# Attention projections from 16-bit high and low parts, and the token transposes moved between the units of k

## The chip, the cores and the metric

The kernel runs on one core of a Trainium2 chip. The metric is the time of one execution on the device in microseconds, from runs of the same compiled program. The engines are called as the profile calls them: PE (TensorE, matmuls), PEld (its weight loads), DVE (VectorE), ACT (ScalarE), POOL (GpSimd) and SP (SyncE, which here only issues DMAs).

## The reference

128 graphs of 128 nodes and 384 features. Each graph is normalised, clipped at zero, and goes through masked attention with 12 heads of 32 features; the input is added to the result.

```python
h = jnp.maximum(_layernorm(x, axis=-1), 0.0)         # x: (128, 128, 384)
q, k, v = (split_heads(h @ W + b) for W, b in ((Wq, bq), (Wk, bk), (Wv, bv)))
scores = einsum('bhqd,bhkd->bhqk', q, k) / sqrt(32) + beta * adj
scores = where(adj > 0, scores, -9e15)
out = x + einsum('bhqk,bhkd->bhqd', softmax(scores), v)
```

All arrays are fp32, and the result is to be close to fp32 arithmetic.

## The kernel before

The graphs are taken four at a time: G = 4 graphs are 512 tokens, and 32 such groups are the steps. Step s projects group s and, in the same time, does the attention of group s-1. 33 steps run in all: step 0 has only projections, step 32 only attention. Each engine runs its own program, and only semaphores tie them together, so the order of instructions on an engine is what its `step` function writes out.

A step is cut into 12 slots, u = 0 to 11. In each slot one chunk of the attention is worked on: a chunk is one graph and CH = 3 chunks of four heads, so 12 chunks for a group. The chunk whose scores are made in slot u is u - 3 (LAG = 3); chunks 9 to 11 of a group thus come in slots 0 to 2 of the step after. A chunk goes through:

- PE: four matmuls into the one score bank `ps_s` (L456), which first waits for DVE to be done with the chunk before
- DVE: four fused instructions that add the mask and take the maximum (L638)
- ACT: four exps (L523)
- PE, one slot later: four transposes of the fp32 probabilities into `ps_t` (L464); ACT copies them as fp16 (L548), and DVE makes the low part, `ps_t` minus that copy, in fp16 (L644)
- PE, a slot later still: twelve small matmuls with v's high and low parts (L479 to L481). After the third chunk of a graph DVE takes the reciprocal of the sums (L654) and scales (L659), POOL adds the input and v's bias (L334), and SP stores

The order on DVE within a slot: L638 for chunk n, then the low parts of the units that PE ended in the slot before (`low_parts`), the reciprocal, one graph's statistics of the next group (L586), the scaling, the mask of the next group (L598 in slot 4, L603 in slot 7), the aggregation of the statistics (L592), and last L644 for chunk n-1. The order on ACT: the exps of chunk n, L548 for chunk n-1, then the high parts of what PE ended in this slot.

Between these, PE works through 13 units, listed in UNITS: three of q, three of k (each 128 output columns for 512 tokens), four of v (one graph each), and three turns. A turn transposes 128 of the 384 normalised features of the next group (L415), and ACT (L530, with the clip at zero) and DVE (L609) split it into a high and a low part, `hT`. A projection unit is 9 matmuls (L435): three blocks of 128 features, each as high x high, low x high and high x low, with both parts kept in fp32 storage as fp32r, which PE multiplies at reduced precision. For q and k the weights are stationary and 512 tokens stream; for v the tokens are stationary and 384 columns stream. ATOMS and PIECES share the 13 units out over the 24 halves of slots by columns (512 or 384 a matmul, 1024 a turn; 44544 in all). Units rotate through three PSUM banks `ps_p`; before a unit starts, `bank_free` waits for what empties the bank's last user: DVE's low part for q, k and turns, ACT's copy for v. The high parts of q and k are made by ACT (L543) and the low ones by DVE (L619), both in fp16; SP spreads them by 12 DMAs each over `q_st` and `k_st` (L248), which the scores read.

POOL computes 1/sqrt(variance) for the next group (L302 to L305) once all its statistics are in, normalises its four graphs (L313), adds v's bias to the input (L319), splits v (L326, L328) and makes the final additions.

Of the kernel before, what the change touches and what calls it, by code (L numbers as in the profile page):

```python
# [5 lines left out]
F32 = mybir.dt.float32  # L6
# [9 lines left out]
EPS = 1e-5  # L16
MASKED = -9000000000000000.0
EXPONENT = 0x7F800000
BINADE = 1 << 23


def graph_attention_kernel(nc, x, adj, wq, bq, wk, bk, wv, bv, beta, out):
# [17 lines left out]
    assert N == P and TOK == 512 and HPC * N == 512  # L40


    UNITS = ([("q", c) for c in range(CH)] + [("k", c) for c in range(CH)]
             + [("v", 0), ("v", 1), ("turn", 0), ("v", 2), ("turn", 1), ("v", 3), ("turn", 2)])
    NB = len(UNITS)
    PROJ = [u for u in UNITS if u[0] != "turn"]
    QK = 2 * CH
    NP = len(PROJ)


# [33 lines left out]
    with ExitStack() as ctx:  # L84
# [3 lines left out]
        def sem(name):  # L88
            return ctx.enter_context(nc.semaphore(name))

        w = sb("w", [P, 2, CH, 3 * D], F32R)
        ones = sb("ones", [P, P], BF16)
        ident = sb("ident", [P, P], F32)
        b_row = sb("b_row", [P, 2, D], F32)
# [18 lines left out]
        rstd = sb("rstd", [P, G], F32)  # L113
        hn = sb("hn", [P, G, D], F32)

        hT = sb("hT", [P, 2, 2, CH, TOK], F32R)
        qT = sb("qT", [P, 2, CH, TOK], FP16)
        kT = sb("kT", [P, 2, CH, TOK], FP16)
        q_st = sb("q_st", [P, 2, HPC, CH, TOK], FP16)
# [167 lines left out]
        @block.gpsimd  # L287
        def _(pool):
            pool.memset(ident[:], 0.0).then_inc(ident_zeroed, 1)
            pool.memset(ones[:], 1.0).then_inc(consts_set, 1)  # L290
            pool.wait_ge(ident_zeroed, 1)
            pool.affine_select(out=ident[:], in_=ident[:], compare_op=ALU.not_equal, fill=1.0, base=0,
                               pattern=[[-1, P]], channel_multiplier=1).then_inc(consts_set, 1)
            pool.memset(half[:], -0.5).then_inc(consts_set, 1)
            pool.wait_ge(consts_set, 3)

            def rstd_of(s):

                wait(pool, var_done, G * (s + 1))
                wait(pool, normed, G * s)  # L300
                pool.nop(nofuse=True)
                pool.tensor_scalar(var_eps[:], mean_var[:, :, 1], EPS, None, ALU.add).then_inc(eps_added, 1)  # L302
                pool.tensor_scalar(neg_mean[:], mean_var[:, :, 0], -1.0, None, ALU.mult).then_inc(eps_added, 1)
                pool.wait_ge(eps_added, 2 * (s + 1))
                pool.tensor_tensor(rstd[:], var_eps[:], half[:], ALU.pow).then_inc(rstd_done, 1)  # L305

            def normalise(s, par):

                pool.wait_ge(rstd_done, s + 1)
                wait(pool, h_turned, CH * s)  # L310
                pool.nop(nofuse=True)
                for j in range(G):
                    pool.tensor_scalar(hn[:, j, :], xs[:, par, j, :], neg_mean[:, j:j + 1], rstd[:, j:j + 1],  # L313
                                       ALU.add, ALU.mult).then_inc(normed, 1)

            def add_bias(s, par, j):
                wait(pool, x_in[par], 8 * (s - par) + 16)
                wait(pool, added, G * (s - 2) + j + 1)
                pool.tensor_tensor(xb[:, par, j, :], xs[:, par, j, :], bv_row[:], ALU.add).then_inc(xb_done, 1)  # L319

            def split_v(s, par, j):
                wait(pool, pv_done, SLOTS * (s - 2) + CH * (j + 1))
                pool.wait_ge(v_copied, G * s + j + 1)
                pool.nop(nofuse=True)
                v32 = v_f[:, j % 2].rearrange("p (h d) -> p h d", d=HD)
                pool.tensor_copy(v1[:, par, j, :, 0:HD], v32).then_inc(v_high, 1)  # L326
                pool.wait_ge(v_high, G * s + j + 1)
                pool.tensor_tensor(v2[:, par, j], v32, v1[:, par, j, :, 0:HD], ALU.subtract).then_inc(v_split, 1)  # L328

            def add_x(s, par, j):  # L330

                pool.wait_ge(scaled, G * s + j + 1)
                pool.wait_ge(xb_done, G * s + j + 1)
                pool.tensor_tensor(on[:, j % 2, :], on[:, j % 2, :], xb[:, par, j, :], ALU.add).then_inc(added, 1)  # L334

            def step(s, par):
                proj, attend = 0 <= s <= STEPS - 1, 1 <= s <= STEPS
                older = 2 <= s <= STEPS
                if 1 <= s <= STEPS:
                    split_v(s - 1, 1 - par, G - 1)  # L340
                if proj:
                    add_bias(s, par, 0)
                    add_bias(s, par, 1)
                if older:
                    add_x(s - 2, par, 2)
                if proj:
                    add_bias(s, par, 2)
                if 0 <= s <= STEPS - 2:
                    rstd_of(s + 1)
                    normalise(s + 1, 1 - par)  # L350
                if older:
                    add_x(s - 2, par, 3)
                if proj:
                    add_bias(s, par, 3)
                if attend:
                    add_x(s - 1, 1 - par, 0)
                if proj:
                    split_v(s, par, 0)
                    split_v(s, par, 1)
                if attend:  # L360
                    add_x(s - 1, 1 - par, 1)
                if proj:
                    split_v(s, par, 2)
                if s == STEPS:
                    add_x(s - 1, 1 - par, 2)
                    add_x(s - 1, 1 - par, 3)

            rstd_of(0)
            normalise(0, 0)
            w_c = w_raw[:, :, W_COLS[1]]  # L370
            pool.wait_ge(w_squared, 2)
            pool.wait_ge(qk_scaling, 9)
            pool.tensor_tensor(w_c, w_c, gap[:, 1:2, :].bitcast(F32).broadcast_to([P, CH, D]),
                               ALU.mult).then_inc(wk_scaled, 1)
            pool.wait_ge(w_squared, 3)
            pool.wait_ge(v_scaling, 6)
            for c in range(CH):
                w_c = w_raw[:, c, W_COLS[2]].rearrange("p (h d) -> p h d", d=HD)
                pool.tensor_tensor(w_c, w_c, v_scale[:].rearrange("p (h o) -> p h o", o=1).broadcast_to([P, HEADS, HD]),
                                   ALU.mult).then_inc(wv_scaled, 1)  # L380
            for par in range(2):
                for j in range(G):
                    pool.tensor_copy(v1[:, par, j, :, HD], v_scale[:]).then_inc(consts_set, 1)
            pool.wait_ge(bv_in, 16)
            run_steps(step)

        @block.tensor
        def _(pe):
            def bank_free(s, par, o):
# [14 lines left out]
                if kind == "turn":  # L404
                    wait(pe, h_low, CH * (before + 1) + n + 1)
                elif kind == "v":
                    wait(pe, v_copied, G * before + n + 1)
                else:
                    wait(pe, qk_low, QK * before + last + 1)

            def turn(s, bank, c):

# [102 lines left out]
        def _(act):  # L515
# [52 lines left out]
                act.activation(w_sq[:, n], w_raw[:, :, W_COLS[n]], ACT.Square).then_inc(w_squared, 1)  # L568
            def weights_high(n, ready, count):
                act.wait_ge(ready, count)  # L570
                act.activation(w[:, 0, :, W_COLS[n]], w_raw[:, :, W_COLS[n]], ACT.Copy).then_inc(w_high, 1)

            weights_high(0, wq_scaled, 1)
            for c in range(CH):
# [7 lines left out]
        def _(dve):  # L582
# [23 lines left out]
            def turn_low(s, par, bank, c):  # L606

                dve.wait_ge(h_high, CH * s + c + 1)
                dve.scalar_tensor_tensor(out=hT[:, par, 1, c, :], in0=bank[:], scalar=0.0,  # L609
                                         in1=hT[:, par, 0, c, :].bitcast(F32), op0=ALU.max,  # L610
                                         op1=ALU.subtract).then_inc(h_low, 1)

            def low_part(s, par, o):

                kind, n = UNITS[o]
                bank = ps_p[BANK[par][o]]
                dve.wait_ge(qk_high, QK * s + o + 1)
                dst, b = (qT, 0) if kind == "q" else (kT, 1)
                dve.scalar_tensor_tensor(out=dst[:, 1, n, :], in0=bank[:], scalar=bias_qk[:, b, n:n + 1],  # L619
                                         in1=dst[:, 0, n, :], op0=ALU.add, op1=ALU.subtract).then_inc(qk_low, 1)  # L620
# [42 lines left out]
            def step(s, par):  # L663
                proj, ahead = 0 <= s <= STEPS - 1, 0 <= s <= STEPS - 2
                for u in range(SLOTS + (LAG + 3 if s == STEPS else 0)):
# [7 lines left out]
                        low_parts(s - 1, 1 - par, SLOTS - 1, s <= STEPS - 1)  # L673
                    if ended:
                        invert_sums(valued[1], valued[3] // CH)
                    if ahead and u < G:
                        moments(s + 1, 1 - par, u)
                    if ended:
                        scale_out(valued[1], valued[3] // CH)
                    if proj and u == 4:  # L680
                        mask_unlinked(s, par)
                    if proj and u == 7:
                        mask_linked(s, par)
                    if ahead and u < G:
                        variance(s + 1, u)
                    if turning:
                        p_low(turning[0], (u - LAG - 1) % 2)

# [33 lines left out]
                              ALU.mult).then_inc(b_scaled_done, 1)  # L722
            def weights_low(n):
                dve.wait_ge(w_high, n + 1)
                dve.tensor_tensor(w[:, 1, :, W_COLS[n]], w_raw[:, :, W_COLS[n]], w[:, 0, :, W_COLS[n]].bitcast(F32),
                                  ALU.subtract).then_inc(w_low, 1)

            turn_low(0, 0, ps_h[0], 0)
            weights_low(0)
# [47 lines left out]
```

## Time and profile before

| | before |
|---|---|
| time, median of 3 runs | 1162.26 us (1161.06 to 1162.73) |
| time of the profiled execution | 1160.99 us |
| its span, first to last instruction | 1159.1 us |
| mean granted TensorE clock | 0.974 |
| busy: PE, PEld, DVE, ACT, POOL | 94%, 78%, 84%, 77%, 50% |
| DMA | 138.79 MB, mean 120 GB/s |

A busy share is the union of an engine's instructions over the span. PE's instructions are pipelined, so they overlap and a busy PE may still be waiting for the next one; DVE and ACT show the length of each instruction with its latency, and the start of the next one may lie before the end of the one before. The distance of two starts is therefore the better measure of what one instruction costs, and it is used throughout.

### The profile page before, as it was taken

Reading aid. Unit: us, or ns where it says so; the run is one execution under the profiler, and the core shown is the slowest. Engines: PE = TensorE matmul, PEld = TensorE weight load, DVE = VectorE, ACT = ScalarE, POOL = GpSimd, SP = SyncE. Lnnn points to the kernel's source line nnn. Section 1 sums busy time; section 2 is a strip of 40 time slices with the busy share of each in tenths; the row PEclk is TensorE's granted clock in tenths of the full one; section 3 lists DMA queues with packets and bytes.
Section 4 is the critical chain, followed back from the end, with each engine's and each line's share of the span. In section 5 each row is a group of like instructions: output and inputs, shape, how many; then the busy total and the mean of one; then the engine's idle time right before and its main releaser. Section 6 shows DMA issues by size and latency. Waiting matters only on the chain. (4 is left out here: it accounts for less than half of the span.)

```text
span 1159.1 us, 33776 instructions
## 1 busy us (share of the span) xinstructions
PE 1089.7 (94%) x10959; PEld 902.9 (78%) x10959; DVE 972.2 (84%) x4343; ACT 891.0 (77%) x2343; POOL 578.6 (50%) x756
## 2 busy tenths in 40 slices
PE   4899999999999999999999999999999999999986
PEld 2778878888878888787888887888888788888764
DVE  6578888888888888898888888888889888888865
ACT  2377888788787888787888878788877888887865
POOL 3735464454555454546545455545454554545331
PEclk9999999999999999999999999999999999999965
DMA  4444434554434455444455443445544444543320
GB/s 145 116 123 123 110 105 123 140 147 126 120 98 123 130 140 136 120 111 113 119 137 147 130 116 100 122 128 139 145 115 109 114 119 134 147 126 98 98 70 28
DMA packets 91038, 138.79 MB, mean 120 GB/s; under 512 B 15600, under 2 KB 66288, under 8 KB 90864
## 3 DMA queue, kind: packets, MB, share of 16 engines
q1 hardware_dynamic: 90336, 135.85, 43.7%
q8 instruction: 88, 1.44, 0.6%
q14 instruction: 86, 0.70, 0.2%
q10 hardware_dynamic: 528, 0.79, 0.2%
HBM read 35.91 MB, written 25.17 MB: 53 GB/s over the span
## 5 line engine op out<-in xcount | busy, mean ns | idle before, releaser
L523 ACT ACTIVATE probs<-biased,neg_max 128x128 f32<-128x128 f32 x1536 | 491.9, 391 | 222.8 <-DVE neg_max L638 186.0
L435 PE MATMUL ps_p<-hT,w 128*128 128x512 f32 x1728 | 527.1, 423 | 5.2 <-DVE qT L619 2.5
L644 DVE TENSOR_TENSOR pT<-ps_t,pT 128x512 f16<-128x512 f32 x384 | 262.9, 685 | 141.3 <-ACT pT L548 141.0
L334 POOL TENSOR_TENSOR on<-on,xb 128x384 f32<-128x384 f32 x128 | 129.2, 1009 | 471.8 <-DVE on L659 392.9
L638 DVE CUSTOM_DVE_ANT_0 biased<-ps_s,mask 128x128 f32<-128x128 f32 x1536 | 352.0, 285 | 6.3 <-PE ps_s L456 4.3
L435 PEld LDWEIGHTS ps_p<-hT,w 128*128 128x128 f32 x1728 | 294.2, 192 | 53.4 <-DVE hT L609 7.3
L435 PE MATMUL ps_p<-w,hT 128*128 128x384 f32 x1152 | 270.2, 357 | 30.4 <-DVE hT L609 30.4
L464 PE MATMUL ps_t<-ident,probs 128*128 128x128 f32 x1536 | 237.8, 279 | 3.1 <-ACT probs L523 1.5
L464 PEld LDWEIGHTS ps_t<-ident,probs 128*128 128x128 f32 x1536 | 193.9, 143 | 43.8 <-ACT probs L523 7.1
L548 ACT ACTIVATE pT<-ps_t 128x512 f16<-128x512 f32 x384 | 220.5, 574 | 1.2 <-PE ps_t L464 1.2
L435 PEld LDWEIGHTS ps_p<-w,hT 128*128 128x128 f32 x1152 | 186.8, 189 | 37.6 <-DVE hT L609 37.5
L479 PEld LDWEIGHTS ps_o<-v,pT 128*128 128x128 f16 x1536 | 122.8, 96 | 84.7 <-issue 73.9
L479 PE MATMUL ps_o<-v,pT 128*128 128x33 f16 x1536 | 160.3, 181 | 3.2 <-DVE pT L644 2.3
L456 PE MATMUL ps_s<-k_st,q_st 96*128 96x128 f16 x1536 | 150.7, 221 | 7.4 <-DVE neg_max L638 4.9
L481 PE MATMUL ps_o<-v,pT 128*128 128x32 f16 x1536 | 155.6, 177 | 0.0
L480 PE MATMUL ps_o<-v,pT 128*128 128x33 f16 x1536 | 155.6, 178 | 0.0
L319 POOL TENSOR_TENSOR xb<-xs,bv_row 128x384 f32<-128x384 f32 x128 | 128.8, 1017 | 8.9 <-POOL on L334 0.4
L638 DVE DVE_READ_ACCUMULATOR2_ANT neg_max<- 128x1 f32 x1536 | 127.7, 83 | 0.1
L480 PEld LDWEIGHTS ps_o<-v,pT 128*128 128x128 f16 x1536 | 125.5, 97 | 0.3
L481 PEld LDWEIGHTS ps_o<-v,pT 128*128 128x128 f16 x1536 | 124.1, 96 | 0.0
L328 POOL TENSOR_TENSOR v<-v_f,v 128x384 f16<-128x384 f32 x128 | 114.0, 891 | 10.3
L456 PEld LDWEIGHTS ps_s<-k_st,q_st 96*128 96x128 f16 x1536 | 90.5, 97 | 10.6 <-DVE neg_max L638 6.2
(62 smaller groups left out, 1034.9 us busy)
## 6 DMA issues: line engine op xcount, KB each, us to landing
q_st<-qT SPq DMA_DIRECT2D x384, 96.0 KB, 2.2
k_st<-kT SPq DMA_DIRECT2D x384, 96.0 KB, 2.2
out<-on SPq DMA_DIRECT2D x128, 192.0 KB, 2.1
xs<-in_x SPq DMA_DIRECT2D x31, 768.0 KB, 4.8
adjs<-in_adj SPq DMA_DIRECT2D x32, 256.0 KB, 5.1
xs<-in_x ACTq DMA_DIRECT2D x1, 768.0 KB, 7.6
k_st<-in_L_gnn_Wq SPq DMA_DIRECT2D x1, 576.0 KB, 5.9
k_st<-in_L_gnn_Wk SPq DMA_DIRECT2D x1, 576.0 KB, 9.2
```

The lines of the kernel that those rows point to most:

```text
L319: pool.tensor_tensor(xb[:, par, j, :], xs[:, par, j, :], bv_row[:], ALU.add).then_inc(xb_done, 1)
L334: pool.tensor_tensor(on[:, j % 2, :], on[:, j % 2, :], xb[:, par, j, :], ALU.add).then_inc(added, 1)
L435: mm = pe.matmul(dst, stationary, moving, start=m == 0, stop=m == MMS - 1)
L456: mm = pe.matmul(ps_s[:, i * N:(i + 1) * N], q_st[0:STACK, gp, i, c, j * N:(j + 1) * N], k_st[0:STACK, gp, i, c, j * N:(j + 1) * N], start ...
L464: mm = pe.transpose(ps_t[odd][:, i * N:(i + 1) * N], probs[:, odd, i, :], ident[:])
L479: pe.matmul(o, high, first, start=True, stop=False)
L480: pe.matmul(o, low, first, start=False, stop=False)
L481: mm = pe.matmul(o[:, 0:HD], high, second, start=False, stop=True)
L523: act.activation(probs[:, odd, i, :], biased[:, odd, i, :], ACT.Exp, bias=neg_max[:, odd, i:i + 1], scale=-1.0).then_inc(exp_done, 1)
L548: act.activation(pT[:, odd, 0], ps_t[odd][:].rearrange("p (h q) -> p h q", q=N), ACT.Copy).then_inc(p_high_done, 1)
L638: dve.tensor_tensor_reduce(out=biased[:, odd, i, :], in0=ps_s[:, i * N:(i + 1) * N], in1=mask[:, gp, v // CH, :], scale=-1.0, scalar=3.0e3 ...
L644: dve.tensor_tensor(pT[:, odd, 1], ps_t[odd][:].rearrange("p (h q) -> p h q", q=N), pT[:, odd, 0], ALU.subtract).then_inc(p_low_done, 1)
```

## The change

The high and low parts of the weights (`w`) and of the tokens (`hT`) are kept in fp16. So that small low parts keep their bits, weights are multiplied by SHRINK = 4 when they are split, and tokens are divided by 4: the variance is multiplied by 16 before the power of -1/2. The products stay as they were. The numbers of matmuls, and the columns in them, stay too. The three turns stand behind k0, k1 and k2 in UNITS instead of between and after the units of v; QK_AT keeps the count of q and k units right. On POOL the 1/sqrt and the normalisation come before `add_x` of graph 2 and `add_bias` of graph 2. On DVE the statistics and their aggregation for four graphs are done two each in slots 0 and 1, where it was one each in slots 0 to 3.

```diff
+SHRINK = 4.0
...
-    UNITS = ([("q", c) for c in range(CH)] + [("k", c) for c in range(CH)]
-             + [("v", 0), ("v", 1), ("turn", 0), ("v", 2), ("turn", 1), ("v", 3), ("turn", 2)])
+    UNITS = ([("q", c) for c in range(CH)] + [(kind, c) for c in range(CH) for kind in ("k", "turn")]
+             + [("v", j) for j in range(G)])
...
+    QK_AT = {o: [u for u in UNITS if u[0] in "qk"].index(unit) for o, unit in enumerate(UNITS) if unit[0] in "qk"}
...
-        w = sb("w", [P, 2, CH, 3 * D], F32R)
+        w = sb("w", [P, 2, CH, 3 * D], FP16)
...
-        hT = sb("hT", [P, 2, 2, CH, TOK], F32R)
+        hT = sb("hT", [P, 2, 2, CH, TOK], FP16)
...
-                pool.tensor_scalar(var_eps[:], mean_var[:, :, 1], EPS, None, ALU.add).then_inc(eps_added, 1)
+                pool.tensor_scalar(var_eps[:], mean_var[:, :, 1], SHRINK * SHRINK, SHRINK * SHRINK * EPS, ALU.mult,
+                                   ALU.add).then_inc(eps_added, 1)
...
+                if 0 <= s <= STEPS - 2:
+                    rstd_of(s + 1)
+                    normalise(s + 1, 1 - par)
                 if older:
                     add_x(s - 2, par, 2)
                 if proj:
                     add_bias(s, par, 2)
-                if 0 <= s <= STEPS - 2:
-                    rstd_of(s + 1)
-                    normalise(s + 1, 1 - par)
...
-                    wait(pe, qk_low, QK * before + last + 1)
+                    wait(pe, qk_low, QK * before + QK_AT[last] + 1)
...
-                act.activation(w[:, 0, :, W_COLS[n]], w_raw[:, :, W_COLS[n]], ACT.Copy).then_inc(w_high, 1)
+                act.activation(w[:, 0, :, W_COLS[n]], w_raw[:, :, W_COLS[n]], ACT.Copy, scale=SHRINK).then_inc(w_high, 1)
...
-                                         in1=hT[:, par, 0, c, :].bitcast(F32), op0=ALU.max,
+                                         in1=hT[:, par, 0, c, :], op0=ALU.max,
...
-                dve.wait_ge(qk_high, QK * s + o + 1)
+                dve.wait_ge(qk_high, QK * s + QK_AT[o] + 1)
...
-                    if ahead and u < G:
-                        moments(s + 1, 1 - par, u)
+                    if ahead and u < 2:
+                        for j in range(2 * u, 2 * u + 2):
+                            moments(s + 1, 1 - par, j)
...
-                    if ahead and u < G:
-                        variance(s + 1, u)
+                    if ahead and u < 2:
+                        for j in range(2 * u, 2 * u + 2):
+                            variance(s + 1, j)
...
-                dve.tensor_tensor(w[:, 1, :, W_COLS[n]], w_raw[:, :, W_COLS[n]], w[:, 0, :, W_COLS[n]].bitcast(F32),
-                                  ALU.subtract).then_inc(w_low, 1)
+                dve.scalar_tensor_tensor(out=w[:, 1, :, W_COLS[n]], in0=w_raw[:, :, W_COLS[n]], scalar=SHRINK,
+                                         in1=w[:, 0, :, W_COLS[n]], op0=ALU.mult, op1=ALU.subtract).then_inc(w_low, 1)
```

## Rows read from the trace of the kernel before

**Rows 1.** The page's part 1: busy us, share of the span, instructions.
```profile
PE 1089.7 (94%) x10959; PEld 902.9 (78%) x10959; DVE 972.2 (84%) x4343; ACT 891.0 (77%) x2343; POOL 578.6 (50%) x756
```

**Rows 2.** Windows: length, busy PE PEld DVE ACT POOL, clock, DMA: 31 steps; last 11 slots.
```profile
60.21:1119.41 1059.20, 1024.34 (x10544) 855.61 (x10542) 916.36 (x4164) 850.84 (x2257) 541.60 (x702) 0.99 0.46 123
1119.41:1150.02 30.61, 24.62 (x221) 16.20 (x220) 18.95 (x106) 19.34 (x55) 2.99 (x3) 0.50 0.08 27
```

**Rows 3.** Timeline of DVE near the end: start, length, engine, line, operation, [idle before].
```profile
1121.59 0.69 DVE L644 TENSOR_TENSOR pT<-ps_t,pT 128x512 f16<-128x512 f32 x1 [1.25 <-ACT pT L548]
1122.19 0.28 DVE L638 CUSTOM_DVE_ANT_0 biased<-ps_s,mask 128x128 f32<-128x128 f32 x1
```

**Rows 4.** Timeline of ACT in the same slot.
```profile
1119.80 1.28 ACT L523 ACTIVATE probs<-biased,neg_max 128x128 f32<-128x128 f32 x4 [1.02 <-DVE neg_max L638]
1120.98 0.57 ACT L548 ACTIVATE pT<-ps_t 128x512 f16<-128x512 f32 x1
```

**Rows 5.** Timeline of DVE in slot u=8.
```profile
519.14 0.28 DVE L638 CUSTOM_DVE_ANT_0 biased<-ps_s,mask 128x128 f32<-128x128 f32 x1
...
519.98 0.75 DVE L619 SCALAR_TENSOR_TENSOR kT<-ps_p,bias_qk,kT 128x512 f16<-128x512 f32 x1
520.65 0.22 DVE L654 RECIPROCAL inv_sum<-ps_o 128x12 f32<-128x12 f32 x1
...
521.38 0.68 DVE L644 TENSOR_TENSOR pT<-ps_t,pT 128x512 f16<-128x512 f32 x1
```

**Rows 6.** Windows of slots inside steps: u=2; u=6; u=7; u=10; u=11, 0, 1.
```profile
501.97:505.14 3.17, 3.17 (x30) 2.46 (x30) 3.17 (x15) 2.34 (x6) 0.50 (x1) 1.00 0.02 5
...
513.57:516.36 2.79, 2.79 (x31) 2.23 (x29) 1.53 (x11) 2.33 (x6) 1.59 (x2) 1.00 0.65 155
516.36:519.14 2.78, 2.78 (x33) 2.58 (x31) 2.78 (x12) 2.33 (x6) 0.00 (x0) 1.00 0.59 153
524.76:527.67 2.91, 1.95 (x26) 1.56 (x25) 2.22 (x11) 2.75 (x8) 1.25 (x2) 1.00 0.64 155
527.67:536.06 8.39, 8.39 (x87) 6.92 (x86) 7.66 (x36) 6.81 (x19) 5.65 (x7) 1.00 0.40 104
```

**Rows 7.** Timeline of PE in slot u=3 of that step.
```profile
504.19 0.38 PE L456 MATMUL ps_s<-k_st,q_st 96*128 96x128 f16 x4
504.38 0.95 PE L435 MATMUL ps_p<-hT,w 128*128 128x512 f32 x3
505.17 0.60 PE L464 MATMUL ps_t<-ident,probs 128*128 128x128 f32 x4
505.52 1.18 PE L435 MATMUL ps_p<-hT,w 128*128 128x512 f32 x4
```

**Rows 8.** Timeline of DVE in slot u=0: low part of turn 2, one graph's statistics.
```profile
531.31 0.69 DVE L609 SCALAR_TENSOR_TENSOR hT<-ps_p,hT 128x512 fp32r<-128x512 f32 x1
531.91 0.55 DVE L586 BATCH_NORM_STATS2 stats<-xs 128x6 f32<-128x384 f32 x1
532.55 0.18 DVE L592 BATCH_NORM_AGGREGATE mean_var<-stats 128x2 f32<-128x6 f32 x1
532.65 0.69 DVE L644 TENSOR_TENSOR pT<-ps_t,pT 128x512 f16<-128x512 f32 x1
```

**Rows 9.** Timeline of PE in slot u=10 and the start of u=11.
```profile
526.34 0.61 PE L435 MATMUL ps_p<-w,hT 128*128 128x384 f32 x2 [0.96 <-DVE hT L609]
527.11 0.38 PE L456 MATMUL ps_s<-k_st,q_st 96*128 96x128 f16 x4
```

**Rows 10.** Timeline of POOL in slots u=3 to 5.
```profile
507.65 0.24 POOL L302 TENSOR_SCALAR var_eps<-mean_var 128x4 f32<-128x4 f32 x1 [0.85 <-DVE mean_var L592]
...
509.55 2.81 POOL L313 TENSOR_SCALAR hn<-xs,neg_mean,rstd 128x384 f32<-128x384 f32 x4 [0.21 <-POOL rstd L305]
```

**Rows 11.** Timelines at the start: SP's issue of k's spreading, PE's first scores.
```profile
49.20 7.53 SPq L248 DMA_DIRECT2D k_st<-kT  x12
...
59.64 0.38 PE L456 MATMUL ps_s<-k_st,q_st 96*128 96x128 f16 x4 [2.53 <-DMA k_st<-kT]
```

## What the change does to the time, predicted before it was run

> **What bounds the kernel now.** I read the page first, then the windows, then the timelines of VectorE (DVE), ScalarE (ACT) and TensorE (PE), slot by slot. On the page PE is busy 94% of the span, DVE 84%, ACT 77% [rows 1]. That invites the reading that PE is the bound. The windows speak against it. The last 11 slots of the kernel have attention and no projection at all. PE has 221 instructions there, against 10544 in the 31 steps before, and its granted clock is 0.50, and yet they take 30.61 us, 2.78 us a slot. The 31 steps with projections take 1059.20 us, 34.17 us a step or 2.85 us a slot [rows 2]. So almost nothing of a slot's length comes from the projections. What sets it is a ring of waits between DVE and ACT, seen bare in one slot of that end: the mask-and-maximum group (L638) starts at 1119.41, where the window begins, the four exps (L523) at 1119.80, ACT's copy of the turned probabilities (L548) at 1120.98, DVE's low part of them (L644, after 1.25 us idle "<-ACT") at 1121.59, the next L638 at 1122.19 [rows 2 to 4]. That is 0.39 + 1.18 + 0.61 + 0.60 = 2.78 us. ACT does the copy of chunk n-1 only behind the exps of chunk n, and DVE the next L638 only behind that L644, so the ring closes without PE.
>
> In a step with projections the same 2.78 us stands under each slot, and a slot is longer only where something exceeds it. Name a slot by the step's own count u (0 to 11); its start is DVE's first L638, and the chunk scored there is u-3. DVE needs 0.84 us for L638 (519.14 to 519.98 [rows 5]) and 0.60 for L644, so 2.78 - 1.44 = 1.34 us fit between them for nothing. In [rows 6] slots u=6 and u=7 take 2.79 and 2.78, u=10 takes 2.91, u=11, 0 and 1 together 8.39 (2.80 each), and u=2 takes 3.17 with DVE busy throughout. Twelve bare slots would be 33.4 us; a step is 34.17 on the mean. Only those 0.8 us a step, and the start and end, are open to this change.
>
> **The change on PE.** First the projections. A run of three fp32 matmuls of 512 columns takes 505.17 - 504.38 = 0.79 us to the next group; one more lengthens the busy time from 0.95 to 1.18, so 0.23 us is one, and the first of a run costs 0.79 - 0.46 = 0.33 [rows 7]. Four fp16 scores of 128 columns take 504.38 - 504.19 = 0.19, which is 0.05 each, so I estimate 0.20 to 0.22 us for 512 fp16 columns and no surcharge for the first. For a step (54 such matmuls, 36 of 384 columns, 24 runs) that is about 54 x 0.02 + 36 x 0.01 + 24 x 0.10 = 3.8 us less work for PE. Its bounds are 0 and 5 us. All of it lies beside the ring. The value for the time is zero, except where PE catches up late: u=11, 0 and 1, where I take 0.05 us a step for all three (8.39 against 3 x 2.78).
>
> By the Trainium skill, page TensorE: Matmul & The Clock Gate, section Back-to-back issue gap, a warm matmul of 512 columns issues every 216 ns; no run so far shows it for fp16, and with it the saving would be about the same. The skill's page Perfetto Trace Analysis, section Identifying the Most-Contended Engine, would rank engines by busy share, with weight loads standing for TensorE. Here that gives DVE at 84% ahead of the weight loads at 78%, but neither share tells of the ring, and the rows decide. By that rule an unchanged total of DVE work would mean an unchanged time, 1162 us.
>
> **The turns move.** Counting columns (44544 a step in 24 halves), before has turn 0 to 2 in u=9, 10 and 11; after has turn 0 in u=5, turn 1 in u=6 and turn 2 in u=8. DVE's low part of a turned chunk (L609, 0.60 us: 531.31 to 531.91 [rows 8]) comes one slot later: before in u=10, 11 and 0, after in u=6, 7 and 9.
> - u=10 loses its stall. There v3 needs the bank of turn 0; PE waits 0.96 us for L609, starts at 526.34, and its scores at 527.11 let the next L638 start only at 527.67 [rows 6, 9]. The slot goes from 2.91 to 2.78: -0.13 us.
> - The same stall reappears in u=6. k2 needs the bank of turn 0, whose L609 is in u=6. PE starts k2 1.58 us into the slot as at u=10 (526.34 - 524.76), has two matmuls there too, of 0.22 each, which is about what two fp32 ones of 384 columns take with the surcharge of the first, and so the slot grows as u=10 did, from 2.79 to 2.91: +0.12 us. Bounds: 0 if the wait just fits, 0.25 if the first matmul keeps its surcharge.
> - u=7 gets three pieces of DVE work: low part of k1 (L619), L609 of turn 1, and the second half of the mask (L603). The slot is full already without L609 (DVE busy for 2.78 of its 2.78 us [rows 6]), so L609's 0.60 comes on top: 3.38 us, +0.60. Bounds 0.55 and 0.65; if fp16 made L609 half as long, 0.3. SP's load of adjs waits for that mask, but behind it SP would wait for an output addition anyway.
> - ACT in u=6 has the high part of k1 and the copy of turn 1; at u=10, with a high part of v and such a copy, it was busy for 2.75 of 2.91 us [rows 6]. k's high part is longer than v's, so this may bind by a little; I take 0, bounds 0 and 0.1.
>
> **The statistics move.** u=2 loses one of the four: it keeps L638, L619, the reciprocal and the scaling (520.65 to 521.38, 0.73) and L644, the same as slot u=8 has now: 0.84 + 0.67 + 0.73 + 0.60 = 2.84 us [rows 5]. It was 3.17: -0.33 us. u=3 loses its statistics as well, worth 0 to 0.07; I take 0.04. Slots 0 and 1 get two each: at most 0.55 + 0.64 + 0.10 = 1.29 us from [rows 8], under the 1.34 that fit, and u=0 has lost the L609 it had. Nothing.
>
> **GpSimd and the queues.** rstd and normalise come before add_x of graph 2 and add_bias of 2. They start when all statistics are in, now in u=1, and turn 0 needs them in u=5, over 10 us on; they take 4.7 us (507.65 to 512.36 [rows 10]). add_x 2, until now in u=3, may come 2 us later; SP's store of it stands ahead of the spreading of q, which waits for q2's low part in u=4 anyway. The variance's multiplication by 16 rides in an instruction that is there already. Nothing, bounds 0 and 0.1 a step.
>
> **The sum.** Per step -0.05 - 0.13 + 0.12 + 0.60 - 0.33 - 0.04 = +0.17 us. It holds for the 30 steps that look ahead and have attention: +5 us. The bounds: -0.3 a step (L609 at half length, no stall in u=6, and u=3 worth 0.07) to +0.4, so -9 to +12 us. At the start, attention waits for the spread of k, issued at 49.20 behind that of q; scores start at 59.64 [rows 11]. The four statistics now stand in pairs ahead of q's low parts and overlap a little, which I put at -0.6 us. Against it, k1 and k2 now stand behind turn 0, which in step 0 waits for GpSimd; I find k2's low part done just before SP is free, so 0, at worst +2. Scaling the weights while splitting them costs the same number of instructions. The end has no projections: nothing. In all 5.1 - 0.6 = +4.5, say +4 us. The profiled execution took 1160.99 us for a span of 1159.1; the median of the three runs lies 1.3 us above it. 1160.99 + 4 = 1165, and 1162.26 + 4 = 1166. I give 1166.
>
> **Rivals.**
> - PE is the bound after all. For it: 94% busy. Against it: the 30.61 us of the last 11 slots. It would give 3.8 us x 31 = 118 us less, 1044 us; chance 0.03.
> - The ring itself gets shorter, since fp16 operands disturb ACT and DVE less. For it: slots with projections show 2.79 to 2.80 instead of 2.78. Against it: that is all there is to gain. 12 x 0.025 = 0.3 us a step, 9 us in all, so 1166 - 9 = 1157; chance 0.14.
> - The two moves cancel: L609 costs less in u=7 than 0.60, or u=6 does not stall. It would give 1160 to 1164, no change; chance 0.18.
> - PE's clock drops, as it now has gaps in each slot. For it: the clock was 0.50 in the last slots, where PE waits for the ring [rows 2]. Against it: in u=10 PE was busy for 1.95 of 2.91 us at clock 1.00 [rows 6], and after the change it would be busy for 2.3 to 2.5 us of nearly every slot. It decides from the point where PE's work at half clock, some 7 projections x 0.44 + 1.9 = 5 us, exceeds the 2.78 of a slot; with two such slots a step it gives 2 x 2.2 x 30 = 132 us, about 1295 us; chance 0.03.
> - Turn 0 holds k up at the start, with the rest as forecast: 1168; chance 0.05.
>
> **How the numbers follow.** The forecast has the remaining 0.57. About 0.2% (2.3 us) is what a measurement of this kernel can tell from no change, so 1160 to 1164.6 is "same". Of the forecast 0.48 lies above and 0.09 in it; the shorter ring is 0.09 faster and 0.05 same; cancelling 0.02 faster, 0.13 same, 0.03 slower. With PE as bound (0.03 faster), the clock (0.03) and the start (0.05) slower, that is 0.14 faster, 0.27 same, 0.59 slower. The range 1157 to 1171 leaves out PE as bound, the clock, and the outer ends of the bounds of both signs.
>
> **What would show it.** In the changed profile: matmuls of 512 columns at about 0.22 us with no surcharge on the first, and PE idle in most slots, waiting for neg_max L638; the last 11 slots still 30.6 us; slot u=2 down to about 2.84, u=10 to 2.78, u=7 up to about 3.39 with DVE busy throughout, u=6 near 2.9 with PE waiting for L609. The prediction is wrong if u=7 stays near 2.8, if plain slots leave 2.78, or if the clock falls below 1.00 inside the steps.

## The result and the profile after

The changed kernel takes 1163.85 us (median of 20 runs, 1162.93 to 1164.96) against 1161.3 us for the kernel before in the same comparison: a ratio of 1.0021, with a 95% interval of 1.0015 to 1.0027. It is slower by a fifth of a per cent, 2.5 us. The profiled execution has a span of 1162.2 us, 3.1 more than before.

The page of the changed kernel, part 1 (compare [rows 1]):

```profile
PE 1050.3 (90%) x10959; PEld 721.8 (62%) x10959; DVE 978.9 (84%) x4343; ACT 892.0 (77%) x2343; POOL 567.9 (49%) x756
```

The weight loads of PE have lost 181 us of busy time and its matmuls 39, and the kernel is slower. DVE's and ACT's shares have hardly moved. The windows, cut at the same events as in [rows 2] and [rows 6] (length, busy PE, PEld, DVE, ACT, POOL, clock, DMA): the 31 steps; the last 11 slots; u=2; u=6; u=7; u=10; u=11, 0 and 1.

```profile
58.98:1122.39 1063.41, 985.57 (x10544) 685.24 (x10541) 923.55 (x4163) 851.83 (x2257) 530.96 (x700) 1.00 0.46 122
1122.39:1153.07 30.68, 24.60 (x221) 16.20 (x220) 18.94 (x107) 19.41 (x55) 2.99 (x3) 0.50 0.08 27
501.99:504.82 2.83, 2.83 (x31) 2.00 (x30) 2.80 (x14) 2.34 (x6) 2.54 (x5) 1.00 0.03 6
513.23:516.12 2.89, 1.59 (x23) 0.98 (x22) 2.22 (x11) 2.50 (x7) 1.55 (x2) 1.00 0.65 156
516.12:519.49 3.37, 3.37 (x38) 2.61 (x36) 3.37 (x13) 2.65 (x7) 0.00 (x0) 1.00 0.64 151
525.12:527.91 2.79, 2.79 (x33) 2.04 (x31) 1.53 (x11) 2.14 (x6) 1.39 (x3) 1.00 0.62 148
527.91:536.28 8.37, 8.03 (x84) 5.38 (x83) 7.71 (x39) 6.63 (x18) 7.16 (x11) 1.00 0.42 107
```

A step is now 34.30 us (1063.41 / 31) instead of 34.17. u=7 has grown from 2.78 to 3.37 with DVE busy throughout, u=6 from 2.79 to 2.89; u=2 has shrunk from 3.17 to 2.83, u=10 from 2.91 to 2.79. What fills u=7 is read from the timeline of DVE there (start, length, engine, line, operation):

```profile
516.12 0.29 DVE L642 CUSTOM_DVE_ANT_0 biased<-ps_s,mask 128x128 f32<-128x128 f32 x1
...
516.97 0.75 DVE L623 SCALAR_TENSOR_TENSOR kT<-ps_p,bias_qk,kT 128x512 f16<-128x512 f32 x1
517.63 0.68 DVE L613 SCALAR_TENSOR_TENSOR hT<-ps_p,hT 128x512 f16<-128x512 f32 x1
518.23 0.75 DVE L607 SCALAR_TENSOR_TENSOR mask<-adjs,beta_col,mask 128x512 f32<-128x512 f32 x1
518.89 0.69 DVE L648 TENSOR_TENSOR pT<-ps_t,pT 128x512 f16<-128x512 f32 x1
519.49 0.29 DVE L642 CUSTOM_DVE_ANT_0 biased<-ps_s,mask 128x128 f32<-128x128 f32 x1
```

Each starts as the one before it lets go: 0.85 + 0.66 + 0.60 + 0.66 + 0.60 = 3.37 us. (Lines are four further down than before: L642 was L638, L648 was L644, L613 was L609, L607 was L603, L439 was L435.) The low part of turn 1 takes 0.60 us as it did in fp32. And PE in u=6 waits for the bank of turn 0, then goes on with the scores of the next chunk at 515.56, which DVE takes up 0.56 us later, at 516.12 (start, length, ..., number of instructions in the group, [idle time before it <- what ended it]):

```profile
514.81 0.61 PE L439 MATMUL ps_p<-hT,w 128*128 128x512 f16 x2 [1.30 <-DVE hT L613]
515.56 0.38 PE L460 MATMUL ps_s<-k_st,q_st 96*128 96x128 f16 x4
515.78 0.81 PE L439 MATMUL ps_p<-hT,w 128*128 128x512 f16 x3
516.43 0.60 PE L468 MATMUL ps_t<-ident,probs 128*128 128x128 f32 x4
516.87 1.03 PE L439 MATMUL ps_p<-hT,w 128*128 128x512 f16 x4
```

### The profile page after: what moved, and what is told of

Read it like the earlier page. It is cut to its first block and busy times, and to the rows that moved or that the text cites. A ratio compares the mean times of both kernels' runs of the same rounds, so it can differ in the third digit from the quotient of the medians.

```text
span 1162.2 us, 33776 instructions
## 1 busy us (share of the span) xinstructions
PE 1050.3 (90%) x10959; PEld 721.8 (62%) x10959; DVE 978.9 (84%) x4343; ACT 892.0 (77%) x2343; POOL 567.9 (49%) x756
## 5 line engine op out<-in xcount | busy, mean ns | idle before, releaser
L439 PE MATMUL ps_p<-hT,w 128*128 128x512 f16 x1728 | 459.0, 382 | 62.0 <-DVE hT L613 38.6
L648 DVE TENSOR_TENSOR pT<-ps_t,pT 128x512 f16<-128x512 f32 x384 | 264.5, 689 | 147.0 <-ACT pT L552 143.6
L642 DVE CUSTOM_DVE_ANT_0 biased<-ps_s,mask 128x128 f32<-128x128 f32 x1536 | 351.7, 286 | 3.5 <-PE ps_s L460 2.5
L338 POOL TENSOR_TENSOR on<-on,xb 128x384 f32<-128x384 f32 x128 | 127.5, 996 | 416.7 <-DVE on L663 416.7
L439 PEld LDWEIGHTS ps_p<-hT,w 128*128 128x128 f16 x1728 | 155.1, 98 | 168.3 <-DVE hT L613 45.9
L439 PE MATMUL ps_p<-w,hT 128*128 128x384 f16 x1152 | 234.4, 326 | 1.3
L483 PEld LDWEIGHTS ps_o<-v,pT 128*128 128x128 f16 x1536 | 132.1, 96 | 48.5 <-DVE pT L648 7.6
L483 PE MATMUL ps_o<-v,pT 128*128 128x33 f16 x1536 | 156.8, 179 | 3.7 <-DVE pT L648 2.8
L484 PE MATMUL ps_o<-v,pT 128*128 128x33 f16 x1536 | 155.6, 178 | 0.0
L484 PEld LDWEIGHTS ps_o<-v,pT 128*128 128x128 f16 x1536 | 125.2, 97 | 35.3
L439 PEld LDWEIGHTS ps_p<-w,hT 128*128 128x128 f16 x1152 | 104.9, 98 | 55.6 <-DVE hT L613 9.6
L323 POOL TENSOR_TENSOR xb<-xs,bv_row 128x384 f32<-128x384 f32 x128 | 127.6, 1008 | 8.9 <-POOL on L338 0.4
L642 DVE DVE_READ_ACCUMULATOR2_ANT neg_max<- 128x1 f32 x1536 | 129.1, 84 | 0.0
L485 PEld LDWEIGHTS ps_o<-v,pT 128*128 128x128 f16 x1536 | 124.1, 96 | 0.0
L330 POOL CAST v<-v_f 128x384 f16<-128x384 f32 x128 | 64.8, 507 | 112.7 <-issue 102.8
```

The costliest lines, as they stand in the source:

```text
L439: mm = pe.matmul(dst, stationary, moving, start=m == 0, stop=m == MMS - 1)
L483: pe.matmul(o, high, first, start=True, stop=False)
L484: pe.matmul(o, low, first, start=False, stop=False)
L485: mm = pe.matmul(o[:, 0:HD], high, second, start=False, stop=True)
L642: dve.tensor_tensor_reduce(out=biased[:, odd, i, :], in0=ps_s[:, i * N:(i + 1) * N], in1=mask[:, gp, v // CH, :], scale=-1.0, scalar=3.0e3 ...
L648: dve.tensor_tensor(pT[:, odd, 1], ps_t[odd][:].rearrange("p (h q) -> p h q", q=N), pT[:, odd, 0], ALU.subtract).then_inc(p_low_done, 1)
```

## The experiments

The theory is the prediction's: a ring between DVE and ACT sets each slot at 2.78 us, and only what exceeds it counts. The main rival is that PE, 90 to 94% busy, is the bound. All ratios are against the kernel before, run on the same chip beside each.

**The fp16 parts alone.** The kernel before with the storage changed (with the factor 4, which is not shown below) and nothing moved:

```diff
-        w = sb("w", [P, 2, CH, 3 * D], F32R)
+        w = sb("w", [P, 2, CH, 3 * D], FP16)
-        hT = sb("hT", [P, 2, 2, CH, TOK], F32R)
+        hT = sb("hT", [P, 2, 2, CH, TOK], FP16)
...
```

> The kernel before with nothing changed but the storage of w and hT (fp16, with the factor 4); turns, statistics and POOL order as before. My theory, the ring of waits between DVE and ACT: every slot keeps its length (u=2 3.17, u=10 2.91, u=7 2.79), except u=11, 0 and 1, where PE was late, which lose up to 0.02 each; with the start, 1 to 3 us less than before, about 1159.5. Rival, PE is the bound: 54 x 0.02 + 36 x 0.01 = 1.4 us a step less, 45 us in all, about 1117. Rival, fp16 operands shorten the ring itself: plain slots under 2.78.

Measured 0.9942 (0.993 to 0.9955), 6.6 us less, against the 1 to 3 expected. Slot u=10, which I had left at 2.91, is shorter. Its timeline on PE, and its window:

```profile
521.70 0.50 PE L437 MATMUL ps_p<-w,hT 128*128 128x384 f16 x2 [1.14 <-DVE hT L611]
522.35 0.38 PE L458 MATMUL ps_s<-k_st,q_st 96*128 96x128 f16 x4
```

```profile
520.12:522.91 2.79, 1.65 (x25) 1.15 (x24) 2.14 (x12) 2.63 (x8) 1.25 (x2) 1.00 0.64 151
```

PE still waits for turn 0's low part and starts 1.58 us into the slot, as in [rows 9]. But from there to the scores it takes 0.65 us (521.70 to 522.35) where it took 0.77, and that is what the slot had over 2.78. So the stall was long enough to show only with fp32 parts: 0.12 x 30 = 4 us. Slots u=0 and u=1 lose 0.06 us a step together (means over the steps), some 2 us. The rest is at the start: the first L638 comes 1.0 us earlier and the first step with attention is 1.3 us shorter, in part as in the changed kernel (below). That makes some 8 us, the difference of the two profiled spans (1159.1 and 1151.1). The saving of PE as a whole (1.4 us a step at the least, 45 us) is not there: the rival of PE as the bound falls.

**The moves alone.** The changed kernel with both tensors back in fp32r.

> The changed kernel with w and hT in fp32 again (no factor 4); turns behind k0, k1, k2, statistics two in u=0 and 1, and POOL order stay changed. Ring theory: u=7 3.37 and u=6 2.89 to 2.95, u=2 2.83, so some 5 us slower than before in the steps, less what fp16 gave at the start: 1163 to 1168. Rival, the loss comes from the fp16 parts: then this kernel is at or under before, 1161.

Measured 1.0075 (1.0062 to 1.0088), 9 us slower, at 1168.47 the upper end of what was expected. Windows of u=6 and u=7:

```profile
516.15:519.19 3.04, 2.62 (x30) 1.97 (x29) 2.22 (x12) 2.65 (x7) 1.57 (x2) 1.00 0.63 151
519.19:522.56 3.37, 3.37 (x36) 2.84 (x35) 3.37 (x13) 2.50 (x7) 0.00 (x0) 1.00 0.59 145
```

u=7 is 3.37 in fp32 too, so its length doesn't come from the type. u=6 is 3.04 instead of 2.89, the same effect of the type as above. The two halves of the change multiply to 0.9942 x 1.0075 = 1.0017, which agrees with the 1.0021 of the whole: the change is a gain of 0.6% from the fp16 parts and a loss of 0.75% from the moves (turns, statistics and POOL's order together).

**The turns put back.** The changed kernel with the old order of units:

```diff
-    UNITS = ([("q", c) for c in range(CH)] + [(kind, c) for c in range(CH) for kind in ("k", "turn")]
-             + [("v", j) for j in range(G)])
+    UNITS = ([("q", c) for c in range(CH)] + [("k", c) for c in range(CH)]
+             + [("v", 0), ("v", 1), ("turn", 0), ("v", 2), ("turn", 1), ("v", 3), ("turn", 2)])
```

> The changed kernel with UNITS as before (turns between the units of v), all else changed. Ring theory: u=7 back to 2.79 and u=6 to 2.79, u=10 up to 2.91, but u=0 now has the low part of turn 2 beside two statistics, 0.84 + 0.60 + 1.16 + 0.60 = 3.20: per step 34.29 - 0.58 - 0.10 + 0.12 + 0.41 = 34.14, about 1159. Rival, the moved turns were for the good and something else costs: slower than 1164.

Measured 0.9948 (0.9935 to 0.996), the same as fp16 alone, and faster than the 1159 us that I expected, in part as u=10 did not go back to 2.91. Slots of one step: u=7 2.79, u=10 2.79, u=0 3.21. So of the moves it is the turns that cost. Moving the statistics, with POOL's order moved too, trades u=2 (3.17 to 2.83) for u=0 (2.79 to 3.21), where turn 2's low part meets two statistics. POOL's order was never changed alone.

**The masks out of the full slot.** The changed kernel with the mask in u=3 and 4:

```diff
-                    if proj and u == 4:
+                    if proj and u == 3:
                         mask_unlinked(s, par)
-                    if proj and u == 7:
+                    if proj and u == 4:
                         mask_linked(s, par)
```

> The changed kernel with the two halves of the mask in u=3 and u=4 instead of u=4 and u=7. Ring theory: u=7 has 0.84 + 0.67 + 0.60 + 0.60 = 2.71 of DVE work and falls from 3.37 to 2.79; u=4 has 0.84 + 0.67 + 0.68 + 0.60 = 2.79 and stays; 0.58 x 31 = 18 us less than the changed kernel, about 1146, under both. Rival, u=7 is long for PE or ACT (two units end in u=6): it stays near 3.3 and the time near 1163.

Measured 0.9909 (0.9894 to 0.9924), 1149.27 us. u=7 is 2.79 as expected, but u=3 grew to 2.91, which was not. The timelines of DVE and of POOL in that slot:

```profile
501.19 0.88 DVE L602 TENSOR_SCALAR mask<-adjs 128x512 f32<-128x512 f32 x1
501.99 0.68 DVE L648 TENSOR_TENSOR pT<-ps_t,pT 128x512 f16<-128x512 f32 x1
```

```profile
499.52 1.30 POOL L317 TENSOR_SCALAR hn<-xs,neg_mean,rstd 128x384 f32<-128x384 f32 x2
500.79 1.00 POOL L338 TENSOR_TENSOR on<-on,xb 128x384 f32<-128x384 f32 x1
```

L602 takes 0.88 us instead of 0.42, and it ends 0.28 us after POOL's L338 does (501.19 + 0.88 = 502.07 and 500.79 + 1.00 = 501.79). So I left L602 in u=4 and moved only L607, to u=6:

> The changed kernel with only the mask's second half (L607) moved, from u=7 to u=6; L602 stays in u=4. With both halves in u=3 and 4, u=3 had grown to 2.90, as L602 took 0.88 us there instead of 0.42 while POOL was at its own L317 and L338. If POOL's work beside it does that, L602 is back to 0.42, u=3 to 2.79, u=6 stays 2.89 (0.84 + 0.60 + 0.68 + 0.60 = 2.72 of DVE work), u=7 2.79: 33.67 a step, some 1146 us, 3 below the version with the masks in u=3 and 4. Rival: L602 is slow in any slot after the move: 1149 or more.

Measured 0.9868 (0.9853 to 0.9883), 1144.86 us, as expected. L602 over all 32 steps, shortest, median and longest in ns, in the version with u=3 and in this one:

```profile
L602 DVE TENSOR_SCALAR mask<-adjs x32: 417/878/1025, 37.4 to 1075.8; 128x512 f32<-128x512 f32 x32
```

```profile
L602 DVE TENSOR_SCALAR mask<-adjs x32: 414/417/1141, 38.0 to 1073.5; 128x512 f32<-128x512 f32 x32
```

With one DVE instruction moved by one slot the changed kernel is 1.3% faster than before instead of 0.2% slower. This is the price of u=7 measured directly: 3.37 - 2.79 = 0.58 us a step, with u=6 still at 2.89.

**Less work for PE.** The kernel before with five of the nine matmuls of each projection unit left out (q, k and v lack most of their low-part products):

```diff
                 for m in range(first, end):
+                    if m % 3 and m != MMS - 1:
+                        continue
```

> The kernel before with 4 of the 9 matmuls of each projection unit (m = 0, 3, 6, 8) and the other five left out, so q, k and v lack most of their low-part products; everything else, its order and the halves they stand in, as before. Ring theory: PE loses 50 of its 90 projection matmuls a step, over 10 us of work, and the time falls only by what PE was late for (u=10 keeps its wait for the bank) and some at the start: 1150 to 1160. Rival, PE is the bound: under 900. Rival, the clock falls since PE has long gaps: granted clock well under 0.97; if PE at half clock fits in 2.78 us a slot the time still stays.

Measured 0.9976 (0.9966 to 0.9985), 2.7 us less, for 1600 matmuls fewer. Page, and windows of the 31 steps, of a bare end, and of the later part of one slot u=0:

```profile
PE 877.8 (76%) x9359; PEld 639.1 (55%) x9359; DVE 968.7 (84%) x4343; ACT 890.4 (77%) x2343; POOL 575.3 (50%) x756
```

```profile
60.00:1115.20 1055.20, 822.54 (x9002) 602.12 (x8999) 912.06 (x4156) 849.33 (x2254) 538.37 (x702) 0.98 0.46 123
1115.20:1145.80 30.60, 24.64 (x221) 16.24 (x220) 18.95 (x106) 19.32 (x55) 2.99 (x3) 0.50 0.08 27
...
562.50:564.46 1.96, 1.70 (x18) 1.40 (x19) 1.46 (x5) 0.82 (x3) 1.88 (x3) 0.59 0.51 155
```

PE is busy 76% instead of 94%, and the steps take 1055 us instead of 1059. That is the plainest evidence that PE does not bind, and it is needed: in the last 11 slots of the kernel before, from which the prediction argued, PE was still busy for 24.62 of 30.61 us, at half the clock [rows 2], while here the clock is 0.98. I had left u=10 its wait for the bank; it fell to 2.78, as with fp16 parts. The run also shows the rival of the clock in small: in the step looked at, PE had waited several times in u=11 and 0, its clock was 0.59 in the last stretch above, and that slot u=0 took 3.28 us instead of 2.80. Ten of 31 steps have a slot u=0 of over 3.1 us, and in eight of them the clock was at its lower level for part of it; the other two are long in the kernel before as well (3.19 and 3.11), at full clock. In the changed kernel u=0 is 2.79 in every step.

**The ring cut.** If the ring is ACT's order (copy of chunk n-1 behind the exps of chunk n), then turning that order round must free the slots. On the kernel before and on the changed one:

```diff
                     scored, turning = (chunk(s, par, u, behind) for behind in range(2))
-                    if scored:
-                        exps(scored[0], (u - LAG) % 2)
                     if turning:
                         p_high(turning[0], (u - LAG - 1) % 2)
+                    if scored:
+                        exps(scored[0], (u - LAG) % 2)
```

> The kernel before with ACT's copy of the turned chunk n-1 (L548) ahead of the exps of chunk n (L523) instead of behind them. Ring theory: the ring of 2.78 us is cut, and a slot becomes the longest of DVE's own work (2.5 us on the mean), PE's own pace with fp32 projections (2.7 to 2.9 where three or four 512-column matmuls stand in a half) and a new ring PE-ACT of 2.4: about 2.75 a slot with fp32, 1110 to 1150 us. Rival, the ring isn't what binds: 1161 or slower.

> The changed kernel with the same exchange on ACT. Ring theory: with fp16 PE's own pace is 2.4 to 2.6, so here the fp16 parts should be worth something at last: slots 2.5 to 2.7 with u=7 at 3.37 still (DVE's own work), 1070 to 1120 us, and under the kernel before with the same exchange by 20 us or more. Rival, fp16 gives nothing anywhere: equal to it.

On the kernel before it gives 0.9981 (0.9972 to 0.999), 1157.18 us, which is less gain than I expected (1110 to 1150). On the changed kernel it gives 0.9481 (0.9465 to 0.9497), 1099.68 us. The profile of the first shows slots well under 2.78 for the first time (u=4 2.44, u=6 2.40, u=9 2.44), but u=10 at 3.37 and u=0 at 3.69 and 3.05 in turn: ACT now sits idle for PE's turned probabilities, and PE had waited for the bank just before. PE and ACT in u=10:

```profile
522.29 0.62 PE L435 MATMUL ps_p<-w,hT 128*128 128x384 f32 x2 [0.41 <-DVE hT L609]
523.07 0.38 PE L456 MATMUL ps_s<-k_st,q_st 96*128 96x128 f16 x4
523.27 1.11 PE L435 MATMUL ps_p<-w,hT 128*128 128x384 f32 x5
524.22 0.60 PE L464 MATMUL ps_t<-ident,probs 128*128 128x128 f32 x4
```

```profile
524.86 0.60 ACT L548 ACTIVATE pT<-ps_t 128x512 f16<-128x512 f32 x1 [0.75 <-PE ps_t L464]
```

So the ring was real: without it slots are shorter than 2.78. Right under it lie two other limits, PE's own pace and its waits for a bank. To know whether fp16 or the moves made the difference, the exchange with fp16 parts and nothing moved:

> The kernel before with fp16 storage of w and hT and the exchange on ACT (L548's copy ahead of the exps), nothing else. Against the same exchange with fp32 parts (1157, slots u=10 and u=0 3.37, ended by PE): if PE sets those slots, fp16 takes 0.3 to 0.5 us off each of u=10, 0 and 2, 1110 to 1135 us. Rival: the gain of the changed kernel with the exchange (1100) came from its moves, and fp16 gives 10 us or less here.

Measured 0.9501 (0.9487 to 0.9515), 1102.34 us. The fp16 parts are worth 55 us once the ring is cut (1157.18 to 1102.34), or 1.8 us a step, but not in the slots where I expected it: u=10 stays at 3.29 (3.37 with fp32) and u=2 at 3.38 (3.32). The gain lies in u=6 (2.39 to 1.55), u=9 (2.43 to 1.93), u=1 (2.65 to 2.45) and u=0 (3.40 to 3.15; all means over the steps). The moves add at most little: the intervals of the two (0.9465 to 0.9497 with them, 0.9487 to 0.9515 without) overlap. Slot by slot they take 1.13 us from u=10, 0.66 from u=3 and 0.50 from u=2, and put 1.35 on u=6 and 0.59 on u=7.

**All together.** First the exchange with the masks in u=3 and 4 and the turns in slots where DVE has room:

```diff
+    UNITS = ([("q", c) for c in range(CH)]
+             + [("k", 0), ("turn", 0), ("k", 1), ("k", 2), ("v", 0), ("turn", 1), ("v", 1), ("turn", 2), ("v", 2), ("v", 3)])
```

> The changed kernel with the exchange on ACT, the masks in u=3 and 4, and the turns where DVE has room and the bank's next user comes two slots later (UNITS: q0 q1 q2 k0 t0 k1 k2 v0 t1 v1 t2 v2 v3). Expected under the exchange alone by up to 0.7 us a step, 1050 to 1100 us, with no slot above 2.85. Rival: DVE's total of 30.4 us a step is already the bound, so moving its work between slots gives nothing.

Measured 0.9304 (0.929 to 0.9318), 1079.23 us. Every second step took 31.7 instead of 31.2, since u=0 alternated: in such steps q0 took over the bank of v2, two units back, whose copy by ACT comes late. PE's first matmuls in such a slot:

```profile
522.92 1.04 PE L439 MATMUL ps_p<-hT,w 128*128 128x512 f16 x4 [0.89 <-ACT v_f L542]
```

So the bank was counted on over the steps, and the masks put in u=4 and 6:

```diff
-    BANK = [[(o + par) % PB for o in range(NB)] for par in range(2)]
...
-                bank = ps_p[BANK[par][o]]
+                bank = ps_p[(s + o) % PB]
```

> fp16 parts, exchange on ACT, turns at u=5, 8 and 10, masks in u=4 and 6, and the PSUM bank of a unit counted on over the steps, so that q0 always follows the unit three back and not at every second step the one two back, whose copy ended u=0 late (3.35 against 2.55). Expected: all steps near 31.0 instead of 31.2 and 31.7 in turn, 1065 to 1075 us.

> The same with w and hT in fp32 again. PE's work in a step is 54 x 0.02 + 36 x 0.011 = 1.5 us more; with the ring cut PE is late in the slots that DVE does not fill, so this should be 1 to 2.5 us a step slower: 1100 to 1140 us. Rival, DVE's total is the bound now: equal within 5 us.

The first takes 1063.75 us, 0.917 (0.9156 to 0.9183) of the kernel before, just under what I expected. u=0 is 2.62 in nearly every step where it was 3.34 and 2.62 in turn; moving the masks took 0.71 us from u=3 and put 0.75 on u=6, so most of the gain over the version before is the bank's. With fp32 parts it is 1113.85 us, 0.9601 (0.9585 to 0.9617): 50 us, or 1.6 us a step, for the type. ACT and DVE in one slot of the fp16 version (here L551 is the copy, L526 the exps, L647 the low part):

```profile
469.70 0.60 ACT L551 ACTIVATE pT<-ps_t 128x512 f16<-128x512 f32 x1 [0.26 <-PE ps_t L467]
470.19 1.27 ACT L526 ACTIVATE probs<-biased,neg_max 128x128 f32<-128x128 f32 x4
```

```profile
470.02 0.68 DVE L612 SCALAR_TENSOR_TENSOR hT<-ps_p,hT 128x512 f16<-128x512 f32 x1
470.62 0.82 DVE L606 SCALAR_TENSOR_TENSOR mask<-adjs,beta_col,mask 128x512 f32<-128x512 f32 x1
471.37 0.68 DVE L647 TENSOR_TENSOR pT<-ps_t,pT 128x512 f16<-128x512 f32 x1
471.97 0.28 DVE L641 CUSTOM_DVE_ANT_0 biased<-ps_s,mask 128x128 f32<-128x128 f32 x1
```

and the windows of its 31 steps, its last 11 slots, and the slot u=7 behind this one:

```profile
59.14:1019.19 960.05, 948.13 (x10540) 661.39 (x10537) 915.84 (x4163) 849.30 (x2256) 530.59 (x699) 1.00 0.50 135
1019.19:1051.78 32.59, 20.67 (x220) 17.07 (x220) 18.93 (x106) 19.34 (x56) 2.98 (x3) 0.50 0.07 25
471.97:474.07 2.10, 2.10 (x27) 1.38 (x26) 2.10 (x12) 1.93 (x7) 0.00 (x0) 1.00 0.32 76
```

In this slot DVE no longer waits for the copy: L647 follows on its own queue. Over the whole run it waited 50 us for it, where it was 141 before. A slot is 2.10 us where DVE has little to do and 2.8 where it is full. Over the steps DVE is busy 915.84 of 960.05 us, 95%, and PE 948.13; that fp32 parts cost 1.6 us a step points to PE as what sets some of the slots now. The last 11 slots went the other way, from 30.6 to 32.6 us. There the exchanged order closes a ring of its own between ACT and PE, which runs at a granted clock of 0.50: PE's transposes wait for the exps, and the next copy waits for the transposes.

```profile
1031.62 1.11 PE L467 MATMUL ps_t<-ident,probs 128*128 128x128 f32 x4 [1.09 <-ACT probs L526]
```

```profile
1032.77 0.60 ACT L551 ACTIVATE pT<-ps_t 128x512 f16<-128x512 f32 x1 [1.20 <-PE ps_t L467]
```

## Why the prediction was right, and where not

The forecast was 1166 with a range of 1157 to 1171, slower by 0.3%; it was slower by 0.21%, 2.5 us where the sum had 4. The mechanism was right: the ring, and the collision in u=7. Two terms were wrong in size, PE's saving and the start. Point by point:

- The bound. Right: the last 11 slots stayed at 30.68 us, PE's relief by itself gave 0.6% where PE as the bound would have given 4%, taking five of nine matmuls away gave 0.24%, and turning ACT's order round gave 5% on the changed kernel.
- u=7, +0.60: measured 2.78 to 3.37, +0.59. u=2, -0.33: measured 3.17 to 2.83, -0.34. u=10, -0.13: 2.91 to 2.79. u=6, +0.12: 2.79 to 2.89, +0.10. u=11, 0 and 1, -0.05: 8.39 to 8.37. With u=3 (2.82 to 2.79, forecast -0.04) the step came to +0.17, and the 31 steps as a whole grew by 1063.41 - 1059.20 = 4.2 us; with the quicker first step taken out (below), the others grew by 0.18 to 0.19 each.
- u=10: right in size, but the reason given was only half. I put the loss of the stall down to the moved turns alone. The fp16 parts alone do it as well, as the stall was 0.12 us too long only with fp32 matmuls behind it. That is why both experiments that left the turns in place came out at 0.994 to 0.995, better than expected.
- What PE saves, 3.8 us a step: wrong by over a third, and with little effect since hardly any of it was on the ring. The term that failed is the surcharge of 0.10 for the first matmul of a run. Behind four scores the first fp32 matmul starts after 0.19 us, the fp16 one after 0.22 (515.56 to 515.78); behind four transposes it is 0.35 ([rows 7]) against 0.44 (516.43 to 516.87). The fp32 one starts earlier and lasts longer. So the surcharge is 0.07 in one case and 0.01 in the other, and PE saves 54 x 0.02 + 36 x 0.01 + 12 x 0.08 = 2.4 us a step. A matmul of 512 fp16 columns takes (516.43 - 515.78) / 3 = 0.217 us. The Trainium skill (page TensorE: Matmul & The Clock Gate, section Back-to-back issue gap) gives about 216 ns as the gap of a single matmul, with which this agrees, and 131 ns for a stream of weight loads and matmuls; no run here comes near the second, and the measurement decides.
- A sign that did not come: I had named PE idle in most slots, waiting for neg_max. In the 31 steps of the changed kernel PE waited for it 28 times, 6.0 us in all, and 38.6 us for the bank of turn 0. PE's busy time contains the latency of its matmuls (four scores are busy for 0.38 us, and the next group starts after 0.22), so short waits don't show in it, and the sign was badly chosen.
- The start, -0.6: measured -1.2, as the first L638 comes at 58.98 instead of 60.21, and then -1.5 more in the first step with attention, 33.16 against 34.63 us, where I had nothing. Of the first part, the moves alone give the 0.6 that I had (first L638 at 59.59), but fp16 alone gives 1.0 (59.23), where I had nothing. Neither is firm, with one profiled execution each: with the turns put back it comes at 60.40. The second part stands in the first two slots, 5.99 against 4.49 us, and most of it goes with PE's clock. Before, PE waited 2.53 us for k's spreading [rows 11], and its clock then fell; after, it waited 0.65 us and the clock held. With fp16 alone the clock held too, after a wait of 2.19 us, and the two slots took 5.02 us; with the turns put back it fell, after 3.31 us, and they took 5.80. The rest is the statistics that no longer stand in the first of them. Windows just after the first L638, of the kernel before and of the changed one:

```profile
60.21:63.00 2.79, 2.79 (x12) 2.04 (x11) 2.32 (x12) 1.85 (x5) 0.00 (x0) 0.61 0.00 0
```

```profile
59.00:62.00 3.00, 3.00 (x21) 1.76 (x19) 2.90 (x18) 2.69 (x9) 3.00 (x5) 1.00 0.00 0
```

In all +5.7 in the steps and -2.7 at the start make the 3.1 of the two spans, where I had +5.1 and -0.6; the larger miss is the start's 2.1 us. The sign held since the collision in u=7, 0.59 x 30 = 18 us, is larger than everything else.
- Turn 0 ahead of k at the start: I had k2's low part done just before SP is free. The timeline of SP shows it came 0.75 us late (the load of adjs issued by 47.56, the spreading at 48.31), which is still 0.9 us earlier than before:

```profile
47.19 0.37 SPq L277 DMA_DIRECT2D adjs<-in_adj  x1
48.31 8.40 SPq L251 DMA_DIRECT2D k_st<-kT  x12
```

## What to carry to other kernels

When an engine is 94% busy, look for a stretch in which it has little to do and see whether the pace changes there, and check it by leaving work of that engine out, as the stretch can differ in other things (here the clock was halved in it). If the pace doesn't change, write down the ring of waits that closes without it: here two in-order queues, ACT and DVE, each with an instruction for chunk n-1 behind those for chunk n. Relief for an engine off the ring is worth little until the ring is cut: the same fp16 parts gave 7 us before the exchange and 50 to 55 after it. And before work is moved, add up each slot of the queue that it comes to: one instruction of 0.6 us in a full slot cost some 18 us, and moving another one out of it gave them back.

## What the runs showed of the hardware

A DVE `tensor_scalar` on fp32 in SBUF (L602, 128x512) took 0.42 us alone and 0.88 us (median) where a POOL `tensor_tensor` on SBUF was under way when it came up. The Trainium skill (page SBUF — State Buffer, section SBUF: two separate sides) says that the two engines share a pair of ports as an exclusive lock, which DVE needs in a two-port mode or with two inputs in SBUF, and that the one that comes second blocks for the whole instruction; the trace agrees, as L602 ended 0.28 us after POOL's instruction. In the kernel before, the same instruction (there L598) came up 0.09 us ahead of POOL's first L313 in most steps and took its 0.42 us. DVE's L648, which reads PSUM, started with POOL's L323 under way (501.99 and 501.93) and took its usual 0.68 us.

fp32r and fp16 matmuls of the same columns differ in pace by less than a tenth: 0.23 against 0.217 us for 512 columns. One of their weight loads takes 0.19 us with fp32r and 0.10 with fp16 (medians), so the changed kernel's PEld is busy for 722 us instead of 903. Whether the longer load has a part in the slower pace was not tested.
